# A decoder layer on one core: a new order for all engines' programs, with norms, scales and turned inputs in finer steps

## What is computed

```python
i, f, g = x @ Wi.T, x @ Wf.T, x @ Wg.T
a = sigmoid(f); b = silu(i) * (1 - a)
h[t] = a[t] * h[t-1] + b[t]                      # linear recurrence over tokens
xg = h * silu(g)
x1 = LN(x + (xg * rsqrt(mean(xg^2) + 1e-5) * w_norm) @ Wo.T)
# WKV with keys x1, values ctx, decay w, bonus u: running sums p (with values) and q
y = (p + e^(u+k) v) / (q + e^(u+k));  x2 = LN(x1 + y)
# MLP with fake-quantised (127 levels per row) inputs, weights and hidden
gate, up = q(x2) @ q(W1).T;  out = LN(x2 + q(silu(gate) * up) @ q(W2).T)
```

## Time and profile before

| | us |
|---|---|
| median of 3 runs (lowest, highest) | 410.21 (410.02, 411.32) |
| the profiled execution's own time | 412.55 |
| its span, first to last instruction | 410.1 |
| busy: PE, PEld, DVE, ACT, POOL | 370.8, 289.9, 353.6, 318.7, 219.3 |
| mean granted TensorE clock | 0.981 |

### The profile page before, as it was taken

One profiled execution on the slowest core, in us unless ns is written; L12 is line 12 of the kernel. 1 busy time (PEld: TensorE's weight loads), 2 busy tenths in 40 slices (PEclk: granted clock), 3 DMA queues, 4 the chain that ended last, 5 costly groups with the idle time before them and its releaser, 6 DMA issues.

```text
span 410.1 us, 7960 instructions
## 1 busy us (share of the span) xinstructions
PE 370.8 (90%) x2774; PEld 289.9 (71%) x2774; DVE 353.6 (86%) x639; ACT 318.7 (78%) x420; POOL 219.3 (53%) x281
## 2 busy tenths in 40 slices
PE   7699899889997899999999999999999999659992
PEld 7698799768964788669775977497749785335541
DVE  3879898888788988988899988998899889898895
ACT  3677599769848989599959996799769994974782
POOL 1546772753355725674377535673566356644561
PEclk9989999999999999999999999999999999959999
DMA  7977456011110013000500050004000300000002
GB/s 257 361 273 269 164 195 243 2 53 27 59 46 0 2 48 134 0 28 2 179 2 27 2 179 2 26 0 154 25 0 26 129 0 0 26 2 18 36 26 77
DMA packets 12842, 31.74 MB, mean 77 GB/s; under 512 B 2038, under 2 KB 5132, under 8 KB 12812
## 3 DMA queue, kind: packets, MB, share of 16 engines
q1 hardware_dynamic: 12812, 31.35, 21.9%
HBM read 27.14 MB, written 4.21 MB: 76 GB/s over the span
## 4 chain that ended last, share of the span: by engine, by line
ACT 25%; PE 24%; issue 15%; DVE 14%; POOL 10%; POOLq 0%; ACTq 0%; DVEq 0%
PE proj_ps L530 13%; PE slot_ps L639 8%; POOL ring L1352 4%; ACT L1056 3%; ACT hqT L1021 2%; ACT ring L1014 2%; ACT L1060 2%; DVE inp L1545 2%; DVE x_max L1670 2%; ACT gate L897 2%; POOL gate L1292 2%; ACT q_state L962 2%; ACT q_state L956 2%; ACT gate L935 1%; ACT xqT L998 1%
## 5 line engine op out<-in xcount | busy, mean ns | idle before, releaser
L639 PE MATMUL slot_ps<-w1q,xqT 128*128 128x512 bf16 (+1 forms) x384 | 83.1, 367 | 5.1 <-DVE ring L1702 2.9
L1352 POOL TENSOR_TENSOR ring<-ring 128x512 f32<-128x512 f32 (+1 forms) x48 | 59.6, 1248 | 42.3 <-ACT ring L1007 41.1
L639 PEld LDWEIGHTS slot_ps<-w1q,xqT 128*128 128x128 bf16 x384 | 36.0, 99 | 44.7 <-issue 4.4
L530 PE MATMUL proj_ps<-x_high,proj_high 128*128 128x256 f32 x384 | 65.3, 292 | 1.7 <-DVE inp L1567 1.0
L530 PE MATMUL proj_ps<-x_high,proj_low 128*128 128x256 f32 x384 | 62.2, 284 | 0.0
L530 PE MATMUL proj_ps<-x_low,proj_high 128*128 128x256 f32 x384 | 62.0, 283 | 0.0
L530 PEld LDWEIGHTS proj_ps<-x_high,proj_high 128*128 128x128 f32 x384 | 53.6, 190 | 3.8 <-issue 1.6
L530 PEld LDWEIGHTS proj_ps<-x_high,proj_low 128*128 128x128 f32 x384 | 53.5, 191 | 0.0
L530 PEld LDWEIGHTS proj_ps<-x_low,proj_high 128*128 128x128 f32 x384 | 53.0, 189 | 0.0
L1327 POOL TENSOR_TENSOR den<-den,q_state 128x512 f32<-128x512 f32 x16 | 21.2, 1328 | 49.3 <-ACT q_state L962 48.9
L1007 ACT ACTIVATE ring<-ring,zero_bias,x_scale 128x512 f32<-128x512 f32 (+1 forms) x48 | 37.0, 775 | 9.5 <-DVE ring L1699 9.4
(11 more groups left out here) (157 smaller groups left out, 835.5 us busy)
## 6 DMA issues: line engine op xcount, KB each, us to landing
ring<-w_gate_up_dram SPq DMA_DIRECT2D x11, 512.0 KB, 4.2
forget<-xT_dram SPq DMA_DIRECT2D x8, 512.0 KB, 3.4
x_sb<-x_dram SPq DMA_DIRECT2D x8, 512.0 KB, 3.8
c_sb<-cT_dram SPq DMA_DIRECT2D x8, 512.0 KB, 4.5
out_dram<-late SPq DMA_DIRECT2D x12, 256.0 KB, 2.1
late<-w_down_dram SPq DMA_DIRECT2D x2, 704.0 KB, 6.9
ring<-w_down_dram SPq DMA_DIRECT2D x2, 704.0 KB, 4.2
scale_rows<-scratch_dram SPq DMA_DIRECT2D x2, 704.0 KB, 6.0
```

Source lines behind the costliest of these rows:

```text
L530: last = nc.tensor.matmul(out, a, b, start=(i == 0), stop=(i == len(terms) - 1))
L639: last = nc.tensor.matmul(slot_ps[:, s, half * 512:half * 512 + width], xqT[:, par, d, t * P:(t + 1) * P], w1q[:, d, half * I + at:half * ...
L1352: nc.gpsimd.tensor_tensor(hid, hid, gate_buf[:, at:at + width], ALU.mult).then_inc(hid_ready, 1)
```

## The change

It has three kinds of edit.

**Finer steps.** `layer_norm_1` becomes `stats_1(b, t)` and `aggregate_1(b)`, `layer_norm_2` likewise; `normalise_1`, `normalise_2`, `split_states` (on DVE) and `turn_inputs` are called for each tile t; `scale_2` becomes `largest_2`, `scale_2`, `invert_2`; `scale_products` becomes `gate_products` and `up_products`; `hidden_scale` gives its second and third operation to `hidden_rec` and `hidden_inv`; `weigh_rows` gives them to `size_rows(q, end)` and `invert_rows(q, end)`, which can serve several loads at once; `mlp_down` is called for 3, 3, 2 and 3 blocks. Apart from the row scales of loads 9 to 11, which are sized and inverted together, no operation is added or dropped.

**Another engine.** The three operations of `biases` go from DVE to GpSimd.

**Another order.** Every list of calls is rewritten, in front of, in and behind the loop, on all five engines. In the first output projection the wait for the low part of the weights stands only in front of the terms that use it.

The core of the diff, without what only renames:

```diff
@@ SP, start @@
-            load_half((0, 0))
             load_xT(0)
             load_rows(0)
+            load_half((0, 0))
             load_half((0, 1))
+            load_rows(1)
...
             load_rows(13)
+            store_scales(0)
+            store_scales(1)
             spread_scales(0)
-            load_x(1)
-            store_scales(1)
-            load_rows(14)
             load_c(1)
             spread_scales(1)
-            load_xT(2)
+            load_rows(14)
+            load_xT(3)
+            store_scales(2)
+            load_c(2)
+            spread_scales(2)
             load_x(2)
@@ PE, start @@
             project(0, 0)
             turn_rows(0)
+            turn_rows(1)
             project(0, 1)
-            turn_rows(1)
...
-            turn_scales(0)
             keep_busy(28)
+            turn_scales(0)
@@ PE, a turn @@
             mlp_up(b, par, 1, [1])
-            mlp_up(b, par, 1, [2])
             turn_values(b + 1, 0)
             turn_values(b + 1, 1)
+            mlp_up(b, par, 1, [2])
             turn_hidden(n, 0, 0)
+            project_out(b + 2, 0)
             turn_hidden(n, 0, 1)
-            project_out(b + 2, 0)
+            mlp_down(n, 0, 0, 3)
             sum_squares(b + 2)
             project_out(b + 2, 1)
-            mlp_down(n, 0, (0,))
-            turn_inputs(b + 1)
-            mlp_down(n, 0, (1,))
+            mlp_down(n, 0, 3, 6)
+            turn_inputs(b + 1, 0)
+            turn_inputs(b + 1, 1)
+            mlp_down(n, 0, 6, 8)
+            mlp_down(n, 0, 8, 11)
@@ PE, end @@
             keep_busy(24, spare)
+            keep_busy(20, spare)
             mlp_up(6, 0, 1, [1])
...
-            keep_busy(20, spare)
@@ ACT, a turn @@
-                normalise_3(n - 3, 1)
             exp_tables()
             exponential(b + 1, 0)
             exponential(b + 1, 1)
             silu_tables()
+                normalise_3(n - 3, 1)
             silu(b, par, 0, [0])
+            silu(b, par, 0, [1])
             read_projection(b + 2, 0)
-            silu(b, par, 0, [1])
+            silu(b, par, 0, [2])
@@ ACT, end @@
             silu(7, 1, 0, [0])
-            read_hidden(13, 1, 0)
             silu(7, 1, 0, [1])
             round_hidden(13, 1, 1)
             silu(7, 1, 0, [2])
-            normalise_3(12, 0)
+            read_hidden(13, 1, 0)
+            normalise_3(11, 1)
@@ POOL, start @@
+            round_rows(0)
+            round_rows(1)
+            biases()
+            round_rows(2)
@@ DVE, a turn @@
+                gate_products(b, 0, 0)
+                up_products(b, 0, 0)
                 hidden_max_row(b - 1, 1)
                 hidden_scale(b - 1, 1 - par, 1)
-                scale_products(b, 0, [0])
-                scale_products(b, 0, [1])
-                scale_products(b, 0, [2])
+                gate_products(b, 0, 1)
                 sum_weights(b + 1, 0)
+                up_products(b, 0, 1)
                 layer_norm_3(n - 2, 0)
+                gate_products(b, 0, 2)
+                up_products(b, 0, 2)
+                hidden_rec(b - 1, 1)
+                hidden_inv(b - 1, 1 - par, 1)
...
                 residual_2(b + 1, 0)
+                split_states(b + 2, 0)
                 residual_2(b + 1, 1)
...
+                split_states(b + 2, 1)
...
+                largest_2(b + 1, 1 - par)
                 mean_square(b + 2)
@@ DVE, start @@
             weigh_rows(4)
+            size_rows(4, 5)
             weigh_inputs(0)
+            invert_rows(3, 4)
             weigh_rows(5)
+            size_rows(5, 6)
+            invert_rows(4, 5)
+            invert_rows(5, 6)
             recurrence(0)
-            split_half((OUT_PROJ, 0))
             gating(0)
+            split_half((OUT_PROJ, 0))
             split_half((OUT_PROJ, 1))
-            split_states(0)
-            biases()
@@ DVE, end @@
             layer_norm_last(14, 0)
+            normalise_last(14, 0)
             read_down(15, 7, 1)
             residual_last(15, 1)
             layer_norm_last(15, 1)
-            normalise_last(14, 0)
             normalise_last(15, 1)
```

602 lines of the change are left out of this document (362 added, 240 removed).

## The result

The changed kernel takes 414.0 us (median of 4 runs, 413.69 to 414.28), the kernel before 410.12 beside it (4 runs, 409.87 to 411.32): ratio 1.0089, 95% interval 1.0067 to 1.011. The forecast was 407.4, within 403.8 to 412.0. Three executions in later jobs, of 937 and 1290 us where all others take about 410, are left out of every ratio.

The account below looks back on a forecast made before the run. PE was taken to bound the loop (busy 41.69 of 42.7 us a turn), with DVE close behind and room mostly outside it. Terms −2.0 − 2.0 + 1.9 − 0.7 = −2.8 on the 410.21 median gave 407.4 us, range 403.8 to 412.0.

Parts of the forecast that it names:

- Start, sum of −0.7 up to the first norm: Start: later first projection and roundings, against biases leaving DVE; first norm's aggregate 0.7 us earlier in all.
- Sum: the first norm's aggregate ends at 48.1: Last step of the start's forecast: the aggregate ends at 48.1 us instead of 48.8.
- the late reciprocals: Start: rows 4 and 5 inverted only behind weigh_inputs(0); their rounding ends near 36.5 to 37, project_out(0) starts near 40.3.
- From 49 to T0, −2.0: From first norm to turn 1's first up-projection product: DVE operations saved or moved bring that product to 129.0, −2.0 us.
- spread_scales(2) ... hidden by 7 us: SP's queue before the loop: the spread behind xT(3) lands near 122, is used at 129, so costs nothing.
- the half-clock stretch of the first projection, 1.7 us: Start: PE first runs at half clock after its later beginning, taken as 1.7 us.
- First turn, −2.0: First loop turn: GpSimd does rstd_1(2) earlier and normalise_3 is absent, so 42.4 us instead of 44.4, −2.0.
- Turns 2 to 5, 43.15: Later loop turns: DVE late behind GpSimd's reordered work, +0.45 us a turn to 43.15, +1.9 in all.
- both waits as forecast: Later turns: DVE's value scan waits for GpSimd about 1 us, PE waits about 1 us ahead of project_out.
- Behind the loop, −0.7: Tail: earlier silu, normalise_last(14) moved ahead, places, keys and exponentials earlier; −0.7 us in all.
- the fillers in one piece (0 ± 1): Tail: second 20 fill transposes ahead of an up-chunk cost 2.2 us cold, but the chunk runs warm; about 0, ±1.
- Rival 2: Late start stays: first norm 4 us later, decided by an aggregate at about 52; 412.2 us in all, chance 0.20.

Follow-up runs that it names:

- e13: Changed kernel with 84 more filler transposes (behind the warm-up, ahead of turn_rows(11) and the first turn_values): 411.78 us, ratio 1.0022 to the kernel before.
- e8: Changed kernel with only the first loads and first roundings of the start in the order of before: ratio 1.0000 to the kernel before.
- e9: e8 with the reciprocals of rows 3, 4 and 5 back where the kernel before has them: ratio 0.9966 to the kernel before.
- e1: Old order on all engines, written with the changed kernel's helpers, biases on VectorE again: 411.82 us, ratio 1.0021 to the kernel before.
- e4: Start and loop in the order of before, only the part behind the loop as changed, in the form of e1: ratio 0.9959 to the kernel before.
- e6: Changed kernel with only the last five transfers of SyncE's start in the order of before: ratio 1.0008 to the kernel before.
- e7: Changed kernel with first part of the start and end of SyncE's start queue as before: 407.02 us, ratio 0.9896 to the kernel before.
- e14: e7 with fillers added ahead of turn_rows(1), turn_rows(11) and the first turn_values: 406.97 us, ratio 0.9893 to the kernel before.
- e5: Changed kernel with only the first part of the start in the order of before, biases still on GpSimd: ratio 0.9914 to the kernel before.

## Why the prediction was wrong

- *Start, sum of −0.7 up to the first norm: wrong, +2.8.* The step that failed is the last one, "Sum: the first norm's aggregate ends at 48.1". The pieces ahead of it were near: first projection 11.97 (12.6), sixth done at 33.4 (32.9), rounding of rows 4 and 5 ended at 37.47 (36.5 to 37). What it had wrong is VectorE's own way to the split of the states. The sum leaves 7.8 us from the output product to the norm instead of 10.5, and that gain was there on VectorE, which sets the norm: 7.4 us from the split's end instead of 10.1, the 2.0 of the biases in it. But a norm at 48.1 then needs a split that ends near 40.7, and it ended at 44.27, 3.6 us later: the whole miss. VectorE began the scan 0.9 us later than before, and its scan, gating, low halves and split took 12.95 us beside GpSimd's roundings and products instead of 8.39. The prediction costed what VectorE does to GpSimd there, and had no term for when VectorE's split ends, with GpSimd's work beside it. The product itself, at 41.74 (40.3), was not what the norm waited for: PE's fillers were done at 41.39, and in e13 it began at 42.80 with the norm at the same place.
- *Within it, the late reciprocals.* Seen at GpSimd (+2 us) and then outweighed by those gains, they measured 3.1 us at the norm (e8 to e9), 0.34% in time, with the first loads as before; in the changed kernel itself they were not undone alone.
- *From 49 to T0, −2.0: half right.* From read 0 to read 1 the changed middle gained 1.5 us in every run. The step "spread_scales(2) ... hidden by 7 us" costed one transfer of the three that were moved: its own landing was hidden, while the x queued behind it was not. That is 1.4 us in turn 1. Ahead of read 0 the stretch from the norm took 42.1 us instead of 40.2; the next point has that.
- *The clock.* No term for a later stretch. I had the half-clock stretch of the first projection, 1.7 us, and e13's rows show that it costs nothing there: TensorE turns rows 1 at 17.80 at full clock and at 17.82 at half, and the rows behind the sixth projection at 33.23 and 33.25. The fall at 76 to 84 us, behind waits that the new order makes, was not considered. The Trainium skill (TensorE: Matmul & The Clock Gate, Part 1) would not fit the warm-up; for the first projection the runs bear it out, by the same rows. The later fall was worth a term: with fillers over both gaps 2.7 us, 0.7%, went, about half of it because x then came in time.
- *First turn, −2.0: wrong.* Read to read it was 44.4 before and after. Behind a start with its x in time it is 43.0, −1.4, so the mechanism was there and the queue took it.
- *Turns 2 to 5, 43.15: right in kind, 42.95 to 43.0 measured,* with both waits as forecast. +1.2 in place of +1.9.
- *Behind the loop, −0.7: too small.* −2.4 in the profiles of before and after and between the runs e1 and e4. Of the first 2.0 lie between read 6 and read 7, where the fillers in one piece (0 ± 1) stand, whose chunk no longer waits; they did more than their term. No run puts a single line of the tail back.
- *Rival 2* (slower, from an aggregate near 52) is what came at the norm (51.66), but only in part by the late roundings it names: they ended at 37.47, 0.5 to 1 us behind the forecast, and it was VectorE that was held. Its price of 412.2 lacked the queue and the clock. Its chance of 0.20 was too low: the text's own output product, 2 us late, spoke for it.

What stays open: how the 3.9 us divide exactly. Single undoings (queue end, fillers, first loads) each took 2.7 to 3.7 us off the ratio and do not add up, since each also decides whether the x is in time and whether the clock falls. The queue's end took 3.3 us off the ratio where its profile is only 0.8 us shorter than the changed kernel's. The changed kernel's four runs lie within 0.6 us, the runs of e6, e8 and e13, with much of the same start, spread over 4.6 to 5.3, so part of each such difference may be in which runs the clock fell. And what separates the two groups of times of the kernel before.

The best version is the changed kernel with the old first part and the old end of SyncE's queue: 407.0 us (e7, e14), 1.0% under the kernel before, 1.9% under the changed one by their ratios.

## What to carry to other kernels

Find which engine's row ends in front of the milestone, and move the milestone by that engine's shift only. Add that engine's shift up from all its operations on the way, each at the length it has beside its new neighbours: here 2.7 us were won behind the split and 5.6 lost ahead of it. When a transfer is moved back in a queue, cost everything that now waits behind it, with the longest transfer in front. And where an order makes TensorE wait a microsecond or two more, look at the granted clock in the next rows: the wait can cost twice, and a few fillers in a run of their own show whether it does: they took 2.7 us off the changed kernel and nothing off the kernel before.

## What the runs showed of the hardware

- Half clock after waits as short as 2.0 us or two of 1.9 and 1.5: 36 fillers took 2.17, 2.78 or 4.04 us at the same place of the program, 28 fillers 1.73 or 3.19. With the same order and the same waits up to there it fell in one profile and not in another: in e5 behind waits of 1.66 and 0.88 us and not in e7 behind 1.67 and 0.88, in e13 behind 2.10 and not in the changed kernel behind 2.10. So one profile can be 1 to 3 us off another of the same start.
- The scales' store of 2.0 KB, transposed on its way, took 7.8 to 10.1 us until it had landed, the 512 KB x behind it 7.2 to 8.0.
- GpSimd's four roundings took 6.05 us beside VectorE's scan and gating, and VectorE's two splits 3.96 to 4.00 us with GpSimd beside them against 1.28; a factor of 3 there. The Trainium skill (SBUF — State Buffer, Who interferes with whom) has one of the two wait for the other's whole instruction. These rows agree with it: the second of the two split instructions took 2.87 us instead of 0.68 and ended 0.5 us behind GpSimd's 2.84 us split of x.
